# Softmax sums from the value product, inverse sums on VectorE, and the last multiply on GpSimd, in a fused attention and expert kernel

## The reference, cut to what matters

```python
h = concatenate([tok(x), txt], axis=1)                  # 32 x 165 x 256
q, k, v = heads(ln(h) @ Wq + bq), heads(ln(h) @ Wk + bk), heads(ln(h) @ Wv + bv)
att = einsum('bhtd,bhsd->bhts', q, k) / 4
att = where(mask == 0, -inf, att)                       # s <= t, and every fourth key dropped
y = einsum('bhts,bhsd->bhtd', softmax(att), v)
h = h + y.transpose(0, 2, 1, 3).reshape(B, T, C) @ Wp + bp
h = h + experts(ln(h))                                  # router, top-k tokens per expert, two layers with gelu
```

## Time and profile before

| | |
|---|---|
| time, median of 3 | 857.08 us |
| profiled execution, its own time | 859.55 us |
| its span | 857.7 us |
| busy: PE, DVE, ACT, POOL | 744.2, 573.1, 397.3, 374.7 us |
| attention rounds 0 to 31, from the first queries to the last mixed values | 68.7 to 475.5 us |
| choice of tokens | about 491 to 567 us |
| experts | about 567 to 857 us |

### The profile page before, as it was taken

How to read it: one execution, slowest core, us unless ns; L and a number is a source line. 1 busy time by engine, 2 the same in 40 slices (tenths; PEclk the granted TensorE clock), 3 DMA queues, 4 the chain that set the end, 5 groups by cost and what they waited for, 6 DMA issues and landing times. The chain is left out here.

```text
span 857.7 us, 18735 instructions
## 1 busy us (share of the span) xinstructions
PE 744.2 (87%) x6840; PEld 673.3 (78%) x6840; DVE 573.1 (67%) x1343; ACT 397.3 (46%) x857; POOL 374.7 (44%) x504
## 2 busy tenths in 40 slices
PE   3699999999999999999997511379999999999994
PEld 2577888888888888888885411369999999999994
DVE  1135777668768768667664378776787787887561
ACT  0214455454455455455443155035557366475570
POOL 3113464464465454465444223023537347355334
PEclk9899999999999999999998755569999999999998
DMA  8952675555774675475661342011344453442122
GB/s 273 307 96 48 89 117 97 86 104 98 108 119 99 94 99 96 103 119 99 96 90 51 94 149 74 29 28 43 72 132 64 117 144 49 127 102 32 34 32 32
DMA packets 80686, 82.36 MB, mean 96 GB/s; under 512 B 36161, under 2 KB 74943, under 8 KB 80244
## 3 DMA queue, kind: packets, MB, share of 16 engines
q1 hardware_dynamic: 67980, 66.92, 38.8%
q0 software_dynamic: 11584, 10.96, 8.2%
q10 hardware_dynamic: 1032, 3.30, 1.1%
HBM read 34.59 MB, written 16.22 MB: 59 GB/s over the span
## 5 line engine op out<-in xcount | busy, mean ns | idle before, releaser
L595 POOL DMA_INDIRECT out<-r_arena x48 | 80.3, 1674 | 118.2 <-DVE r_arena L1530 107.9
L656 ACT ACTIVATE r_arena<-ps_all 126x660 f32<-126x660 f32 x128 | 92.2, 720 | 56.9 <-PE ps_all L879 55.3
L1249 DVE RECIPROCAL r_arena<-ps_all 128x165 f32<-128x165 f32 x64 | 76.1, 1189 | 61.3 <-PE ps_all L894 61.3
L520 POOL TENSOR_SCALAR_AFFINE_SELECT r_arena<-r_arena 126x660 f32<-126x660 f32 x128 | 97.0, 767 | 45.9 <-ACT r_arena L656 45.5
L1238 DVE TENSOR_REDUCE mx<-ps_all 128x4 f32<-128x504 f32 (+1 forms) x160 | 105.0, 669 | 15.3 <-PE ps_all L856 13.8
L879 PE MATMUL ps_all<-Qp,Kp 98*126 98x166 f32 x512 | 84.6, 289 | 7.9 <-ACT r_arena L656 6.1
L856 PE MATMUL ps_all<-Kp,Qp 96*65 96x56 f32 (+1 forms) x512 | 90.6, 293 | 0.0
L1552 DVE TENSOR_TENSOR hT_lo<-r_arena,hT_hi 128x330 fp32r<-128x330 f32 x128 | 63.2, 502 | 39.8 <-ACT r_arena L760 39.6
L582 POOL DMA_INDIRECT xe<-xn_rows,r_arena x48 | 59.8, 1245 | 63.4 <-issue 36.5
L1111 PE MATMUL ps_all<-xeT_hi,W_hi 128*128 128x330 f32 x256 | 83.1, 325 | 1.1 <-DVE hT_lo L1552 1.1
L758 ACT ACTIVATE hT_hi<-ps_all,vec_s 128x330 fp32r<-128x330 f32 x128 | 68.9, 539 | 32.4 <-PE ps_all L1111 30.1
(11 more groups left out here) (178 smaller groups left out, 1706.6 us busy)
## 6 DMA issues: line engine op xcount, KB each, us to landing
H<-w SPq DMA_DIRECT2D x16, 1024.0 KB, 5.6
Qp<-q_hi SPq DMA_DIRECT2D x64, 166.0 KB, 3.9
Kp<-k_hi SPq DMA_DIRECT2D x128, 63.0 KB, 4.1
Qp<-q_lo SPq DMA_DIRECT2D x32, 166.0 KB, 4.7
out<-H SPq DMA_DIRECT2D x16, 330.0 KB
xn_rows<-r_arena SPq DMA_DIRECT2D x16, 330.0 KB
Kp<-k_lo SPq DMA_DIRECT2D x64, 63.0 KB, 4.1
H<-h SPq DMA_DIRECT2D x1, 3360.0 KB, 22.6
```

The costliest lines, as they stand in the source:

```text
L520: pool.affine_select(PT[0:S, g, :, :], PT[0:S, g, :, :], [[0, 4], [STEP - 1, T]], ALU.is_ge, 0.0, base=STEP - 2, channel_multiplier=-STEP) ...
L595: pool.indirect_dma_start(rows_out, bass.IndirectOffsetOnAxis(tok[0:A, e % NTB, a:a + 1], 0), yw[0:A, a, :], None, bounds_check=NTOK - 1, ...
L656: act.activation(PT[0:S, g, :, :].rearrange("p (k h) t -> p k h t", k=2), pair[:, :, :, 0:T], ACT.Exp, scale=float(HD) ** -0.5).then_inc(e ...
L1249: dve.reciprocal(rS[:, c, :], bank(2 + c)[:, T:2 * T]).then_inc(rs_sum, 1)
```

## The change

`mix_values` makes one product per head. Its weights are 32 wide: each head's 16 values with a one behind each, so that even partitions of the strip hold values and odd partitions the sums. The two heads of a strip go into columns 0 to 164 (w = 0) and 165 to 329 (w = 1). ACT copies each half c from PSUM to `y_raw`; DVE takes the reciprocal of all of it, values too, into `y_inv`; two transfers on SP's queue bring the second head's values onto the odd partitions of `y_raw` and the first head's inverse sums onto the even partitions of `y_inv`; and POOL multiplies in the rounds' next turn. Rows of `Wp` and of `bv` are permuted to match. The packed keys `Kp` have the head pair's index outside of the head's, so that a row of 1008 bytes of `k_hi` or `k_lo` lands as one piece where it was two of 504.

```diff
-            Qp, Kp = sb1("Qp", [128, 3, HC, TE], F32R), sb1("Kp", [128, 3, HC, 2, S], F32R)
+            Qp, Kp = sb1("Qp", [128, 3, HC, TE], F32R), sb1("Kp", [128, 3, 2, HC, S], F32R)
-            V = sb1("V", [128, 3, 2, 272])
+            V = sb1("V", [128, 3, NH, HD, 2])
+            y_inv = sb1("y_inv", [128, 2, KD, T])
...
 SP
+            def move_heads(b):
+                sp.wait_ge(y_inverse, 2 * b + 2)
+                sp.dma_start(y_raw[1:128:2, 0], y_raw[0:128:2, 1]).then_inc(y_moved, 16)
+                sp.dma_start(y_inv[0:128:2, 1], y_inv[1:128:2, 0]).then_inc(y_moved, 16)
...
                 if 0 <= b + 1 < B:
                     pack_max(b + 1)
+                if 0 <= b < B:
+                    move_heads(b)
                 if u == 1 and 0 <= n - 1 < NPAIR:
                     store_h(n - 1)
...
 POOL
+            def heads_out(b, c):
+                n, u = divmod(b, 2)
+                pool.wait_ge(y_moved, 32 * b + 32)
+                apart(pool)
+                if n >= 2 and c == 0 and u == 0:
+                    pool.wait_ge(proj_done, RT * (n - 2) + RT)
+                    apart(pool)
+                pool.tensor_tensor(yT[:, n % 2, c, u * T:(u + 1) * T], y_raw[:, 0, c, :], y_inv[:, 1, c, :], ALU.mult)\
+                    .then_inc(yT_ready, 1)
...
                 if u == 0:
...
                     if has_s:
                         zero_future(b, 1)
+                        if b >= 1:
+                            heads_out(b - 1, 0)
+                            heads_out(b - 1, 1)
                         zero_future(b, 2)
                 else:
...
                     if has_s:
                         zero_future(b, 0)
                         zero_future(b, 1)
+                        heads_out(b - 1, 0)
+                        heads_out(b - 1, 1)
                     if 0 <= n - 1 < NPAIR:
                         norm_weight(n - 1)
...
 ACT, at the end of each round
+            def copy_heads(b, c):
+                act.wait_ge(pv_done, 2 * b + c + 1)
+                if b >= 1:
+                    act.wait_ge(yT_ready, 2 * b + c - 1)
+                act.activation(y_raw[:, :, c, :], bank(2 + c)[:, 0:2 * T].rearrange("p (w t) -> p w t", w=2), ACT.Copy)\
+                   .then_inc(y_copied, 1)
...
 PE, mix_values
-                    pe.wait_ge(yT_ready, 2 * b + c - 1)
+                    pe.wait_ge(y_copied, 2 * b + c - 1)
                 for w in range(2):
-                    for part in range(2):
-                        for j in range(4):
-                            dst = bank(2 + c)[32 * j:32 * j + 32, part * T:(part + 1) * T]
-                            lhs = v_rows(b % 3, w, 4 * c + j)[0:S] if part == 0 else ones_eo[0:S, w, :]
-                            mm = pe.matmul(dst, lhs, PT[0:S, 2 * c + w, j, :], start=(w == 0 and part == 0),
-                                           stop=(w == 1), skip_group_check=True)
+                    for j in range(4):
+                        mm = pe.matmul(bank(2 + c)[32 * j:32 * j + 32, w * T:(w + 1) * T],
+                                       V[0:S, b % 3, 2 * (4 * c + j) + w].rearrange("p d o -> p (d o)"), PT[0:S, 2 * c + w, j, :], start=(w == 0),
+                                       stop=(w == 1), skip_group_check=True)
...
 DVE, in the place of its heads_out
-                dve.wait_ge(pv_done, 2 * b + c + 1)
-                dve.reciprocal(rS[:, c, :], bank(2 + c)[:, T:2 * T]).then_inc(rs_sum, 1)
...
+            def invert(b, c):
+                dve.wait_ge(y_copied, 2 * b + c + 1)
+                if b >= 1:
+                    dve.wait_ge(yT_ready, 2 * b + c - 1)
+                dve.reciprocal(y_inv[:, :, c, :], y_raw[:, :, c, :]).then_inc(y_inverse, 1)
```

## The result

The changed kernel takes **983.12 us** (median of 4 runs, 980.98 to 986.04) against 857.27 (4 runs, 855.34 to 858.67): 1.147 times as long (95% interval 1.144 to 1.151), or 126 us more. The prediction was 945, its range 888 to 985. The profiled run took 980.98; its span is 979.2.

A forecast was written before the change was run, and what follows sets the result against it. PE was fullest (93%), beside a nearly equal DVE-POOL chain that the change lengthens: even rounds +47.5 and +1.2, odd +32.9 and +1.8, rounds 0 and 1 -1.5, end +6.4; together +88, so 945 us (888 to 985).

The forecast's parts named there:

- O: The end of the odd round's first half of mixed values, forecast 14.33 us after the even round's (11.98 before).
- rival C: DVE's reciprocal out of SBUF runs at twice the rate, 1.1 us each: 883 us; chance 0.08.
- 48-column row: A DVE reciprocal of 48 columns from SBUF, 453 ns, used to price 330 columns at 2.15 us.
- D: Rival: PE's clock falls in the new holes before `project`, 48 us more, 993 us; chance 0.10.
- DVE's 1.86: Odd round: the statistics start 1.86 us later behind the copy and two longer reciprocals, 5.05 us after the half, not 3.19.
- A: Main case: the longer chain over DVE and POOL delays PE, 945 us, own range 925 to 968; chance 0.62.
- PE busy was forecast near 68%: Sign that the main forecast is right: PE busy near 68% in the rounds.
- matmuls at twice their time: Sign on PE that the main forecast is wrong and D holds.
- B: Rival: POOL's multiplies find room and only DVE is late, 895 us; chance 0.12.
- E: Rival: PE stays the bound, DVE's and POOL's additions go into their idle time, 842 us; chance 0.08.

The follow-up runs named there:

- e12: e4 with POOL's list in the order of e3; 836.21 us, 0.973 of the kernel before.
- e1: The changed kernel with 24 small bf16 products, read by nobody, in each of PE's two long holes; 954.3 us, ratio 1.115.
- e7: The kernel before with DVE's reciprocals over all 330 columns out of PSUM instead of the 165 of sums; 939.22 us, ratio 1.095.
- e3: The changed kernel with POOL's multiplies ahead of add_bp in even rounds and at the end of odd rounds; 914.86 us, ratio 1.067.
- e9: The changed kernel with transfers before 165-column reciprocals, inverted next round behind low_q and low_k, and multiplies moved on POOL's list; 914.4 us, ratio 1.066.
- e4: The changed kernel with reciprocals over 2 x 8 and multiplies over 8 columns after the first images, most normalisation left out; 855.33 us, ratio 0.998.
- e8: e3 with copy_logits between the two reciprocals of an odd round instead of behind them; 921.33 us, ratio 1.073.

## Why the prediction was right, and where it was not

**The delays and their chain: right.** In the pair shown, E, the end of the even round's first half, is 375.89 + 0.57 = 376.46. The statistics start at 381.41, E+4.95 (forecast 5.05); `norm_weight` ends at 387.11 + 2.10 = 389.21, E+12.75 (forecast 12.83). With O at about 391.30 + 0.8 = 392.1, the even round has its statistics at 397.14, O+5.0 (5.15), the multiplies' end at 404.99, O+12.9 (13.17), and `project` at O+12.95 (13.3). The parts alone confirm the names: reciprocals 81, multiplies 25, and no cost of copies and transfers that shows (e12). With the clock held up (e1), a pair takes 31.2 against the forecast 31.5.

**Sizes within the chain.** The reciprocal takes 2186 ns, two in 4.29 (4.3 forecast); rival C, at twice the rate, is out. (The working's argument against C was weaker than it read: the 48-column row "lies on the slow line" because the line was drawn through it.) The Trainium skill ("VectorE: DVE Perf Modes", the perf-mode tier table) grants the double rate only to operations with a program for it, and lists no reciprocal; the trace agrees as far as it goes, with no double rate here: 2186 ns out of SBUF, 2216 out of PSUM (e7). A multiply took 0.48 alone and two 0.91 (0.53 and 1.06 forecast), while `norm_weight` took 2.10 for 1.83, so the two errors nearly cancel. The transfers landed in 1.9 us where 3.2 was taken; POOL waited for one in round 1 and in the last pair alone, so in the rounds between they were hidden either way. PE's product lost what was said, 1.14 to 0.57 a half.

**The failed step: "D, PE's clock falls in the new holes … Against it: the holes are 2.7, and the ones of 0.8 before changed nothing."** The holes of about 2 us did change it, behind 21 of the 26 within 8 us. I had only rows of 0.8 and 4.03 on either side and put 0.10 on the far side's effect. A second part of the same step was wrong: I counted one long hole in a pair, before `project`, and about 1 us before `transposes2`. DVE's 1.86 in the odd round shows up as a whole, as a hole of 1.96 at the third row scores, and there too the clock fell, so `transposes2` and the half behind it ran slow: E to O took 15.6 instead of 14.33. From `project` to the half's end took 410.66 - 405.05 = 5.6 instead of 3.88. Together some 3 us in this pair; e1 measures 29 us in all. D had 3.7 a pair from one hole, 48 in all: the right mechanism, but each hole slows fewer steps than D had, there are two of them in a pair, and not each has the effect. D's price also rested on a misread row: behind the hole of 4.03 in the kernel before, a pair of transposes was slow (1.36 for 0.73), but the three projection tiles were not; the 2.81 us of the earlier trace rows ran at a clock of 1.00. D's 993 was A's delays plus the clock. It lies nearer to the measured 983 than A's 945, and A's own range ended at 968; the stated range holds 983 because it took in some of D. The Trainium skill ("TensorE: Matmul & The Clock Gate", section "HAM oscillation — how this bites in real kernels") describes a loop in which a wait in every tile puts the clock back down in every tile; the trace agrees in kind, with 0.60 and 0.73 in the stretches of the pair above, though not in every pair and hole.

**The rest of the 38 us.** e1's 29 leave 9. About 4 of them are no cost of the change: the profiled execution before was 2.5 above its median, the one after 2.1 below, and between the profiled ones the forecast was +88 and the measured is +121, a miss of 33. The rounds at both ends took 22 us more, where the forecast had 16. Part is the last pair, whose `project` came behind a hole of 5.00, at half clock:

```profile
595.81 4.95 PE L928 MATMUL ps_all<-W_s,r_arena 128*110 128x256 f32 x12 [5.00 <-POOL r_arena L530]
```

The same twelve products took 2.81 before: 2.1 us. And the hole of 4.03 before the last scores became 5.68. The rest I can't assign.

**Two signs named ahead.** PE busy was forecast near 68% and measured 84%: the steps at half clock count as busy, and the 93% of the earlier trace rows are of a stretch that the last rounds thin out (100 to 400 us: 99%). And "matmuls at twice their time" was named as a sign of D: the first projection tile behind the hole at 235.91 took 2.04 for 1.05.

**A wait that the working did not see.** The keys of the next image wait for `copy_logits`, which stands behind both reciprocals: up to 1.06 us in an even round (4.9 us in 9 of them from 100 to 400). In the changed kernel it cost nothing that I can tell, since POOL's chain was later; it came out in e3, once POOL's order was mended (8.8 us in 7 waits).

**Rivals.** B (DVE alone, 895) is out: multiplies alone cost 25. Its price for DVE's part was low as well, as e7 costs 81. E (PE stays the bound, 842) is out, but e12 at 836 shows that its gain is there once neither DVE nor POOL is late.

## What to carry to other kernels

A full engine isn't the only bound: here PE was 93% busy, and a delay of 4.1 us a pair on an engine with 30% idle time came through at 3.7 in e7 before the clock added to it. Half of DVE's idle time lay ahead of what started the chain and not behind it (in the kernel before, 40 of 80 us from 100 to 400, right before the reciprocals). So before work goes from a full engine to emptier ones, write down where each added instruction stands in its in-order list, and what waits for the instruction behind it; moving two multiplies within POOL's list was worth 68 us of 126. And price a new hole in PE twice: once for its length, once for the slower clock that may follow, here 29 us of 126; a test with small products in the holes tells which part is which.

## What the runs showed of the hardware

- In a PE that was busy otherwise, holes of 1.90 to 2.34 us were followed by a granted clock of 0.50 to 0.71 over the next 4 us in 17 of 26 cases (changed kernel, 100 to 530 us), and by full clock in 9. Holes of 1.55 to 1.57 in e9 were followed by a lower clock in 9 of 28 cases, from 100 to 500 us. Behind the holes of 0.80 to 1.27 us of e3, e4 and e8 in the rounds from 100 us on it was full each time.
- 24 small bf16 products in the hole (2.06 us) kept the clock up: 0.98 against 0.86 over 100 to 400 us, and 954 us against 983.
- A reciprocal of 128x330 took 2186 ns out of SBUF and 2216 out of PSUM; 166 columns 1192. The source makes almost no difference here, the number of columns nearly all.
- The two transfers between partitions of SBUF landed in 1.8 to 3.9 us, median 1.9, though they go from every other partition to every other.
- Packets of twice the size in the keys' transfers (12,288 fewer in all) changed the time by 0.3% (0.0 to 0.5%), so their number cost little here.
